# A maximum over partitions moves from two turns on the tensor engine to one instruction on GpSimd

## The chip, the cores and the metric

The kernel runs on one core of one Trainium2 chip. The metric is the time of one execution on the device, in microseconds (us). The kernel before was run three times: 1069.85, 1070.06 and 1070.55 us, median 1070.06. One further execution was taken by the hardware profiler; everything called a row below comes from it.

The engines of a core have short names here: PE is the tensor engine's matrix multiply and PEld its loading of weights, DVE the vector engine, ACT the scalar engine, POOL is GpSimd, SP the engine that issues the transfers. Each works through its own queue in order, and they meet at semaphores.

## What is computed

Two layers over an input of 32 sequences of 256 tokens with 128 channels, all in fp32. Layer 0 is a spin attention gated by a small recurrent feed-forward part. Layer 1 is a retention over 16 heads, gated by a soft mixture of 8 experts with 64 slots each. The change is in the mixture:

```python
logits = jnp.einsum('bnd,esd->bnes', xn, sn)
dispatch = jax.nn.softmax(logits, axis=1)
combine = jax.nn.softmax(logits.reshape(b, n, e * s), axis=-1)
slots = jnp.einsum('bnd,bnes->besd', xn, dispatch)
h = jnp.einsum('besd,edh->besh', slots, w1) + b1[None, :, None, :]
h = jax.nn.gelu(h, approximate=False)
eo = jnp.einsum('besh,ehd->besd', h, w2) + b2[None, :, None, :]
eo = eo.reshape(b, e * s, DIM)
out = jnp.einsum('bmd,bnm->bnd', eo, combine)
```

`combine` is a softmax over the 512 slots of each token, so it needs each token's largest logit.

## The kernel before

**Tiling and stages.** The work is done in 16 pairs of sequences (512 tokens). What a pair needs is cut into named steps, such as `("quad", 3)`, scores of four heads of the retention, or `("h", 5)`, first layer of expert 5. For each of PE, DVE, ACT and POOL the table `ORDER` lists the steps of one turn as (name, index, age). `steps_of` (L226) walks it: in turn t an engine does each listed step for pair t minus age. So one turn holds layer 0 of a new pair (age 0), most of layer 1 of the pair before it (age 1) and the last of layer 1 of the one before that (age 2). There are 18 turns for 16 pairs. The order is fixed when the program is written; at run time an engine only waits on semaphores in that order. The table `BANK` says which of four PSUM banks a step of PE fills.

**The retention's chain.** For each q of 0 to 7: POOL scales the keys (`km`, L320), PE makes the scores (`quad`, L1000 and L1003), DVE applies the causal mask (`ret`, L659), ACT takes the absolute value (`ab`, L479), POOL adds one block onto another (`add`, L326), and PE multiplies with the values (`g`, L1023, done for two q at a time: `g` 4 and `g` 5 stand side by side, 24 matrix instructions each in the trace). `ms` (L1030) follows. There are two buffers of `ret` and `ret_abs`, and four of `km`.

**The mixture.** PE makes the logits with slots on partitions and tokens along the row: four tiles `LT` (L930), which ACT copies to `cT` (`LTc`, L440). The dispatch softmax goes `DTe` (ACT, L455), `drec` (DVE, L723), `dn` (POOL, L333), `DT` (four turns on PE, L952), `Dc` (ACT). Then `slots` (L960), and for each expert `h` (L969), `hb` (DVE), `hg` (ACT, Gelu, L474) and `eo` (L979).

**The token maximum.** In `cT` the slots of a token lie across partitions and over the four tiles. DVE takes the maximum of the four tiles (`mx`, three instructions, L707). To get over the partitions, PE turns the result, four instructions (`mxT`, L938), DVE reduces each row and negates it (`rmax`, L712), PE turns it back spread over all partitions, four instructions (`rB`, L945), and ACT copies it out of PSUM (`rBc`, L445). DVE adds it to each tile (`cs`, L719), ACT takes the exponential (`ce`, L449), and `out` (L989) uses it. `out` waits for `ce` 3.

**Layer 0.** Between these stand `s` (L845), `k` (L890), `global` (L840), `score` (L856, two), `r` (L884), `PT` (L866, two), `srow` (L825), `v` (L896), `local` (L876). POOL makes the reciprocal roots of the layer norms (`rstd`, `rstd2`, `rnorm`), with a power instruction each; `xn2T` on PE waits for `rstd2` over DVE's `xn2`.

## Time and profile before

| | |
|---|---|
| median of three runs | 1070.06 us |
| the profiled execution's own time | 1069.8 us |
| its span, first to last instruction | 1068.0 us |
| busy PE / PEld | 1040.6 / 822.9 us |
| busy DVE / ACT / POOL | 918.3 / 810.7 / 414.8 us |
| mean granted clock of the tensor engine | 0.996 of full |

The span is what the rows are measured in; 1.8 us of the execution lie outside it. Busy time counts the instructions that compute. Matrix instructions overlap on PE, and the profile models their ends, so their durations add up to more than they take: the spacing of their starts, or the pieces of the chain of waits, tell what one step costs. The steady part of the execution repeats itself to within some hundredths of a microsecond from pair to pair.

### The profile page before, as it was taken

The numbers are of one execution on the slowest core, as the hardware profiler recorded it, in microseconds if no ns is written. First come the engines' busy times: TensorE is split into PE (matmuls) and PEld (weight loads), VectorE is DVE, ScalarE is ACT, GpSimd is POOL, SyncE is SP. The second block draws the span as 40 slices with busy tenths as digits, with TensorE's granted clock in tenths as the row PEclk, the third lists the DMA queues.
The fourth block names the chain that finished last, engine by engine and source line by source line (L and its number), as shares of the span: only waits on it lengthen the run. The fifth ranks groups of instructions, "written<-read, shape, count | busy, mean of one in ns | idle before, by whom it ended". The sixth has DMA issues, their size and how long they took to land.

```text
span 1068.0 us, 27273 instructions
## 1 busy us (share of the span) xinstructions
PE 1040.6 (97%) x10244; PEld 822.9 (77%) x10244; DVE 918.3 (86%) x1818; ACT 810.7 (76%) x1434; POOL 414.8 (39%) x555
## 2 busy tenths in 40 slices
...
DMA packets 18463, 16.85 MB, mean 16 GB/s; under 512 B 800, under 2 KB 17440, under 8 KB 18080
## 3 DMA queue, kind: packets, MB, share of 16 engines
...
## 4 chain that ended last, share of the span: by engine, by line
PE 94%; DVE 2%; issue 1%; ACT 1%; POOL 0%; DVEq 0%; ACTq 0%; POOLq 0%
PE bank L1023 13%; PE bank L979 11%; PE bank L969 11%; PE bank_s L1000 7%; PE bank L989 6%; PE bank L960 5%; PE bank L930 5%; PE bank L825 3%; PE bank L856 3%; PE bank L923 3%; PE bank L910 3%; PE bank L952 3%; PE bank_s L1003 3%; PE bank L876 3%; PE bank L1030 3%; PE bank L1038 2%
## 5 line engine op out<-in xcount | busy, mean ns | idle before, releaser
L326 POOL TENSOR_TENSOR ret_abs<-ret_abs 128x512 f32<-128x512 f32 x128 | 181.4, 1421 | 250.5 <-ACT ret_abs L479 250.3
L659 DVE TENSOR_TENSOR ret<-bank_s,k_sb 128x1536 f32<-128x1536 f32 x128 | 223.7, 1748 | 29.5 <-PE bank_s L1003 19.9
L479 ACT ACTIVATE ret_abs<-ret 128x1536 f32<-128x1536 f32 x128 | 189.7, 1482 | 26.8 <-DVE ret L659 26.8
L979 PEld LDWEIGHTS bank<-w_sb,hact 128*128 128x128 f32 x1024 | 127.9, 191 | 18.0 <-issue 7.8
L979 PE MATMUL bank<-w_sb,hact 128*128 128x128 f32 x1024 | 138.6, 278 | 0.0
L333 POOL TENSOR_SCALAR dT<-dT,drec 128x256 f32<-128x256 f32 x128 | 67.2, 542 | 170.2 <-DVE drec L723 170.2
L969 PE MATMUL bank<-slotsT,w_sb 128*128 128x128 f32 x1024 | 130.1, 275 | 0.4 <-ACT slotsT L469 0.4
L969 PEld LDWEIGHTS bank<-slotsT,w_sb 128*128 128x128 f32 x1024 | 123.2, 192 | 1.7 <-ACT slotsT L469 0.8
L474 ACT ACTIVATE hact<-hact 128x512 f32<-128x512 f32 x128 | 80.1, 627 | 52.1 <-DVE hact L728 51.8
L1023 PE MATMUL bank<-ret,vrow 128*32 128x256 f32 (+1 forms) x2048 | 108.2, 329 | 0.3 <-POOL ret_abs L326 0.3
L1000 PE MATMUL bank_s<-qT,km 32*128 32x256 f32 x1024 | 91.4, 426 | 0.9 <-POOL km L320 0.6
L1023 PEld LDWEIGHTS bank<-ret,vrow 128*32 128x32 f32 x2048 | 59.9, 109 | 42.0 <-issue 2.5
L728 DVE TENSOR_TENSOR hact<-bank,v_sb 128x512 f32<-128x512 f32 x128 | 87.4, 683 | 4.5 <-PE bank L969 2.4
L320 POOL TENSOR_SCALAR km<-kT,k_sb 128x256 f32<-128x256 f32 x128 | 76.1, 606 | 37.5 <-DVE kT L645 37.5
L1023 PE MATMUL bank<-ret_abs,k_sb 128*32 128x256 f32 x1024 | 78.7, 379 | 0.0
L455 ACT ACTIVATE dT<-cT,ltmax 128x256 f32<-128x256 f32 x128 | 63.8, 505 | 7.1 <-PE bank L952 5.9
L1000 PEld LDWEIGHTS bank_s<-qT,km 32*128 32x128 f32 x1024 | 40.0, 182 | 37.5 <-issue 32.6
L440 ACT ACTIVATE cT<-bank 128x512 f32<-128x512 f32 x64 | 38.4, 600 | 35.7 <-PE bank L989 27.5
L989 PE MATMUL bank<-eorow,cT 128*128 128x129 f32 x512 | 61.4, 278 | 1.0 <-issue 1.0
L989 PEld LDWEIGHTS bank<-eorow,cT 128*128 128x128 f32 x512 | 58.4, 191 | 3.0 <-issue 1.2
L739 DVE TENSOR_TENSOR eorow<-bank,v_sb 64x256 f32<-64x256 f32 x128 | 53.6, 419 | 5.5 <-PE bank L979 4.5
L960 PE MATMUL bank<-d,xn 128*128 128x512 f32 x128 | 57.7, 593 | 0.0
...
## 6 DMA issues: line engine op xcount, KB each, us to landing
...
w_sb<-w SPq DMA_DIRECT2D x2, 2048.0 KB, 13.8
...
k_sb<-consts SPq DMA_DIRECT2D x1, 538.0 KB, 5.9
...
```

The source lines that it names most:

```text
L320: pool.tensor_scalar(km[:, q % KM], kT[par][:, b], K["head"][:, i:i + 1], 1.0, ALU.mult, ALU.mult)\
L326: pool.tensor_tensor(both[:, :, P:SEQ], both[:, :, P:SEQ], both[:, :, SEQ:3 * P], ALU.add)\
L474: act.activation(hact[:, e % 2], hact[:, e % 2], ACT.Gelu).then_inc(ready["hg"].sem, 1)
L479: act.activation(ret_abs[:, q % MR], ret[:, q % MR], ACT.Abs).then_inc(ready["ab"].sem, 1)
L659: dve.tensor_tensor(ret[:, q % MR], bank_s[:, :, 0:3 * P], causal.unsqueeze(1).broadcast_to([P, Q, 3 * P]), ALU.mult)\
L728: dve.tensor_tensor(hact[:, e % 2], bank[:].rearrange("p (c n) -> p c n", c=HC), V["b1"][:, e * HC:(e + 1) * HC].unsqueeze(2).broadcast_to ...
L960: ins = pe.matmul(bank[:], xn3[:, j], d[:, j], start=(i == 0), stop=(i == 1))
L969: ins = pe.matmul(bank[:, c * P:(c + 1) * P], w1_sb[:, e, c * P:(c + 1) * P], slotsT[:, e // 2, 2 * (e % 2):2 * (e % 2) + 2].rearrange("p ...
L979: ins = pe.matmul(bank[:, i * C:(i + 1) * C], hact[:, i, c], w2_sb[:, e, c], start=(c == 0), stop=(c == HC - 1))
L989: ins = pe.matmul(bank[:, i * (C + 1):(i + 1) * (C + 1)], cT[:, m, j * P:(j + 1) * P], eorow[:, m, b], start=(m == 0), stop=(m == E // 2 - 1))
L1000: pe.matmul(bank_s[:, n, 0:SEQ], km[rows, q % KM, 0:P], qT[par][rows, b], start=True, stop=True)
L1023: ins = pe.matmul(bank[n * HT:(n + 1) * HT, into[0]:into[1]], left, src[:, q % MR, n, cols[0]:cols[1]], start=(i == 0 and phase == 0), sto ...
```

## The change

GpSimd takes the maximum over partitions itself. In the function `rBc`, now on POOL, `partition_all_reduce` writes to every partition of `rB` the maximum over the 128 partitions of `mx`.
```diff
--- before.py
+++ after.py
 ORDER = {
...
-    "POOL": [("rnorm", 0, 1), ("add", 6, 2), ("add", 7, 2), ("rstd", 0, 0), ("km", 0, 1), ("km", 1, 1),
...
+             ("km", 5, 1), ("add", 2, 1), ("km", 6, 1), ("km", 7, 1), ("add", 3, 1), ("rBc", 0, 1), ("add", 4, 1),
+             ("add", 5, 1), ("rstd2", 0, 0), ("rnorm", 0, 0), ("add", 6, 1)],
...
@@ -139,7 +139,7 @@
         snT_turned = slot_sb[:].rearrange("p j c -> p (j c)")
         slot_n = sb("slot_n", 3, 4)
         mu1, gamma2, warm = sb("mu1", 2), sb("gamma2", 1), sb("warm", 1)
-        mhalf, ln_eps = sb("mhalf", HEADS), sb("ln_eps", TILES)
+        mhalf, ln_eps, spare = sb("mhalf", HEADS), sb("ln_eps", TILES), sb("spare", 2)
         W = {n: w_sb[:, a:b] for n, (a, b) in W_COLS.items()}
         V = {n: v_sb[:, a:b] for n, (a, b) in V_COLS.items()}
         K = {n: k_sb[:, a:b] for n, (a, b) in K_COLS.items()}
@@ -180,7 +180,7 @@
 
         cT = sb("cT", 4, TOK)
 
-        mx, rmax, rB = sb("mx", TOK), sb("rmax", TILES), sb("rB", TOK)
+        mx, rB = sb("mx", TOK), sb("rB", TOK)
         crec = sb("crec", TILES)
         ltmax, dsum, drec = sb("ltmax", 4, 2), sb("dsum", 4, 2), sb("drec", 4, 2)
         dT, d = sb("dT", 2, 2, SEQ), sb("d", TILES, ES)
@@ -326,6 +326,15 @@
                 pool.tensor_tensor(both[:, :, P:SEQ], both[:, :, P:SEQ], both[:, :, SEQ:3 * P], ALU.add)\
                     .then_inc(ready["add"].sem, 1)
 
+            def rBc(p, par, k):
+
+
+                pool.partition_all_reduce(spare[:, 0:1], mhalf[:, 0:1], P, bass.bass_isa.ReduceOp.max)
+                pool.wait_ge(*ready["mx"](p, 2))
+                since(pool, ready["cs"], p - 1, 3)
+                pool.partition_all_reduce(rB[:], mx[:], P, bass.bass_isa.ReduceOp.max).then_inc(ready["rBc"].sem, 1)
+                pool.tensor_tensor(spare[:, 1:2], mhalf[:, 0:1], mhalf[:, 0:1], ALU.add)
+
             def dn(p, par, m):
                 pool.wait_ge(*ready["drec"](p, m))
                 pool.sem_inc(passed["gpsimd"].sem, 1)
@@ -344,7 +353,7 @@
                 pool.tensor_tensor(slot_n[:, 2], slot_n[:, 1], mhalf[:, 0:4], ALU.pow).then_inc(ready["slot_rn"].sem, 1)
 
             steps_of({"rstd": rstd_, "mixa": mixa, "rstd2": rstd2_, "rnorm": rnorm_, "km": km_,
-                            "add": add, "dn": dn}, ORDER["POOL"],
+                            "add": add, "rBc": rBc, "dn": dn}, ORDER["POOL"],
                      between={("rstd", 0): derived, ("mixa", 0): slot_norms})
 
         @block.scalar
@@ -439,11 +448,6 @@
                 since(act, filled["out"], p - 1, 1)
                 act.activation(cT[:, m], bank[:], ACT.Copy).then_inc(ready["LTc"].sem, 1)
 
-            def rBc(p, par, k):
-                bank = bank_of("rB", p)
-                since(act, ready["cs"], p - 1, 3)
-                act.activation(rB[:], bank[:], ACT.Copy).then_inc(ready["rBc"].sem, 1)
-
             def ce(p, par, m):
                 act.wait_ge(*ready["cs"](p, m))
                 act.activation(cT[:, m], cT[:, m], ACT.Exp).then_inc(ready["ce"].sem, 1)
@@ -514,7 +518,7 @@
                         .then_inc(ready["slot_ready" if j < 3 else "slot_sqs"].sem, 1)
 
             steps_of({"xnTc": xnTc, "sT": sT_, "sgT": sgT_, "eTc": eTc, "P": P_, "PTc": PTc, "sp": sp_, "tr": tr, "kr": kr, "tv": tv,
-                           "xn2Tc": xn2Tc, "xn3Tc": xn3Tc, "LTc": LTc, "rBc": rBc, "ce": ce, "DTe": DTe, "Dc": Dc, "slc": slc,
+                           "xn2Tc": xn2Tc, "xn3Tc": xn3Tc, "LTc": LTc, "ce": ce, "DTe": DTe, "Dc": Dc, "slc": slc,
                            "hg": hg, "ab": ab, "gTb": gTb, "usq": usq_, "dsq": dsq, "ln": ln, "rs": rs, "zt": zt_}, ORDER["ACT"],
                      between={("eTc", 0): slot_squares})
 
@@ -701,22 +705,16 @@
             def mx_(p, par, i):
                 dve.wait_ge(*ready["LTc"](p, i + 1))
                 if i == 0:
-                    since(dve, filled["mxT"], p - 1)
+                    since(dve, ready["rBc"], p - 1)
                 else:
                     dve.wait_ge(*ready["mx"](p, i - 1))
                 dve.tensor_tensor(mx[:], mx[:] if i else cT[:, 0], cT[:, i + 1], ALU.max).then_inc(ready["mx"].sem, 1)
-
-            def rmax_(p, par, k):
-                bank = bank_of("mxT", p)
-                since(dve, filled["rB"], p - 1)
-                dve.tensor_reduce(rmax[:], bank[:].rearrange("p (j s) -> p j s", j=TILES), X, ALU.max, negate=True)\
-                   .then_inc(ready["rmax"].sem, 1)
 
             def cs(p, par, m):
                 dve.wait_ge(*ready["rBc"](p))
                 dve.wait_ge(*ready["DTe"](p, m))
                 dve.wait_ge(*ready["mx"](p, 2))
-                dve.tensor_tensor(cT[:, m], cT[:, m], rB[:], ALU.add).then_inc(ready["cs"].sem, 1)
+                dve.tensor_tensor(cT[:, m], cT[:, m], rB[:], ALU.subtract).then_inc(ready["cs"].sem, 1)
 
             def drec_(p, par, m):
                 dve.wait_ge(*ready["DTe"](p, m))
@@ -791,7 +789,7 @@
             steps_of({"stat": stat_, "xn": xn_, "mix": mix_, "gbias": gbias_, "srowc": srowc, "smax": smax_,
                            "srec": srec_, "field": field, "ka": ka_, "rv": rv_, "rvg": rvg, "prod": prod, "x1": x1_,
                            "stat2": stat2_, "xn2": xn2_, "xn3": xn3_, "qkc": qkc, "vgc": vgc, "ret": ret_, "den": den_, "ug": ug_,
-                           "rx": rx_, "gated": gated_, "attn": attn_, "LTm": LTm, "mx": mx_, "rmax": rmax_, "cs": cs, "drec": drec_, "hb": hb, "eoc": eoc,
+                           "rx": rx_, "gated": gated_, "attn": attn_, "LTm": LTm, "mx": mx_, "cs": cs, "drec": drec_, "hb": hb, "eoc": eoc,
                            "z": z_, "zg": zg, "sg": sg, "x2": x2_}, ORDER["DVE"],
                      between={("stat", 0): derived, ("smax", 1): slots_scaled, ("stat2", 0): slots_turned})
 
@@ -930,20 +928,6 @@
                     ins = pe.matmul(bank[:, b * SEQ:(b + 1) * SEQ], (snT[:], snT_turned)[b][:, m * P:(m + 1) * P],
                                     xn3T[:, b * SEQ:(b + 1) * SEQ], start=True, stop=True)
                 ins.then_inc(filled["LT"].sem, 1)
-
-            def mxT(p, par, k):
-                pe.wait_ge(*ready["mx"](p, 2))
-                bank = claim("mxT", p)
-                for j in range(TILES):
-                    ins = pe.transpose(bank[:, j * P:(j + 1) * P], mx[:, j * P:(j + 1) * P], ident)
-                ins.then_inc(filled["mxT"].sem, 1)
-
-            def rB_(p, par, k):
-                pe.wait_ge(*ready["rmax"](p))
-                bank = claim("rB", p)
-                for j in range(TILES):
-                    ins = pe.transpose(bank[:, j * P:(j + 1) * P], rmax[:, j:j + 1].broadcast_to([P, P]), ident)
-                ins.then_inc(filled["rB"].sem, 1)
 
             def DT(p, par, m):
                 pe.wait_ge(*ready["dn"](p, m))
@@ -1054,7 +1038,7 @@
 
             steps_of({"xnT": xnT_, "s": s, "global": global_, "e": e, "srow": srow_, "score": score, "PT": PT,
                           "local": local, "r": r, "k": k_, "v": v, "xn2T": xn2T_, "xn3T": xn3T_, "qk": qk, "vg": vg, "LT": LT,
-                          "mxT": mxT, "rB": rB_, "DT": DT, "slots": slots, "h": h, "eo": eo, "out": out_, "quad": quad, "g": g,
+                          "DT": DT, "slots": slots, "h": h, "eo": eo, "out": out_, "quad": quad, "g": g,
                           "gT": gT, "ms": ms, "o": o}, ORDER["PE"],
                      between={("s", 0): weights_in, ("local", 0): slots_across, ("xn2T", 0): slots_in})
 
```

What moved, in the order of instructions. POOL, middle of a steady turn: `km`, `add` and `dn` of one pair before the change.

```order
L320 TENSOR_SCALAR km<-kT,k_sb 128x256 x2
L326 TENSOR_TENSOR ret_abs<-ret_abs 128x4x128 x2
L333 TENSOR_SCALAR dT<-dT,drec 128x256 x2
L326 TENSOR_TENSOR ret_abs<-ret_abs 128x4x128 x2
L320 TENSOR_SCALAR km<-kT,k_sb 128x256
L299 TENSOR_TENSOR var_eps<-mv,ln_eps 128x4
L301 TENSOR_TENSOR rstd<-var_eps,mhalf 128x4
```

The same place after the change. The two ISA rows without operands load a library; the one with `spare` is the one-column reduction.

```order
L320 TENSOR_SCALAR km<-kT,k_sb 128x256 x2
L326 TENSOR_TENSOR ret_abs<-ret_abs 128x4x128
L332 ISA
L332 ISA spare<-mhalf 128x1
L335 ISA rB<-mx 128x512
L336 ISA
L336 TENSOR_TENSOR spare<-mhalf 128x1
L326 TENSOR_TENSOR ret_abs<-ret_abs 128x4x128 x2
L299 TENSOR_TENSOR var_eps<-mv,ln_eps 128x4
L301 TENSOR_TENSOR rstd<-var_eps,mhalf 128x4
L306 TENSOR_TENSOR rn<-rstd 128x4
```

The reduction and its two library loads now stand between `add` 3 and `add` 4 of a pair, once for each pair; all `km` and `dn` of the pair stand ahead of them, and `add` 4, `add` 5, `rstd2` and `rnorm` behind.

PE before the change, from `g` 0 and `g` 1 over `quad` 3 to `ms` 0.

```order
L1023 MATMUL bank<-ret_abs,k_sb 32x256 x4
L938 MATMUL bank<-k_sb,mx 128x128 x4
L845 MATMUL bank<-sT,w_sb 128x512
L890 MATMUL bank<-mix,w_sb 128x512
L1000 MATMUL bank_s<-qT,km 128x256 x4
L1003 MATMUL bank_s<-qT,km 128x128 x4
L952 MATMUL bank<-k_sb,dT 128x128 x4
L945 MATMUL bank<-k_sb,rmax 128x128 x4
L1030 MATMUL bank<-usq,k_sb 128x256
```

PE after the change, from `local` (L874 now) over `quad` 5 (L984, L987), `ms` 1 (L1014), four steps each of `h` (L953) and `eo` (L963), `quad` 6, to `g` 4 (L1007).

```order
L874 MATMUL bank<-srow,probT 128x128 x8
L984 MATMUL bank_s<-qT,km 128x256 x4
L987 MATMUL bank_s<-qT,km 128x128 x4
L1014 MATMUL bank<-usq,k_sb 128x256
L953 MATMUL bank<-slotsT,w_sb 128x128 x4
L963 MATMUL bank<-w_sb,hact 128x128 x8
L953 MATMUL bank<-slotsT,w_sb 128x128 x8
L963 MATMUL bank<-w_sb,hact 128x128 x8
L984 MATMUL bank_s<-qT,km 128x256 x4
L987 MATMUL bank_s<-qT,km 128x128 x4
L1007 MATMUL bank<-ret,vrow 32x256 x4
```

The turns by L938 and L945 are gone. Between `quad` 3 and `g` 4 of a pair PE now has `vg` 1, `h` 2 to 4 and `eo` 0 to 3 more than before, and `DT` 1, `rB`, `o` 1 and `global` less.

On DVE and ACT, `cs` and `ce` 1 to 3 have moved from the end of a pair's age-1 turn into its next turn. There PE's order up to `out` is `eo` 5, `h` 7, `ms` 2, `g` 6, `g` 7, `eo` 6, `eo` 7, `ms` 3, `qk` 0, `xn3T`, `qk` 1, and ACT's ends with `hg` 7, `usq` 3, `ce` 1, `dsq` 3, `ce` 2, `ce` 3.

## Rows read from the trace of the kernel before

**Rows 1.** The page: busy time of PE; engines' shares of the chain.

```profile
PE 1040.6 (97%) x10244; PEld 822.9 (77%) x10244; DVE 918.3 (86%) x1818; ACT 810.7 (76%) x1434; POOL 414.8 (39%) x555
...
PE 94%; DVE 2%; issue 1%; ACT 1%; POOL 0%; DVEq 0%; ACTq 0%; POOLq 0%
```

**Rows 2.** Windows, 64 us: busy PE, PEld, DVE, ACT, POOL; clock, DMA.

```profile
454.00:518.00 64.00, 64.00 (x640) 50.80 (x636) 56.85 (x113) 50.00 (x90) 25.85 (x34) 1.00 0.04 10
```

**Rows 3.** Groups of PE: busy us, mean ns of one, idle before.

```profile
L938 PE MATMUL bank<-k_sb,mx 128*128 128x128 f32 x64 | 10.5, 286 | 0.0
```

**Rows 4.** Chain of waits, 504 to 569 us: start, length, step.

```profile
504.83 0.58 PE bank L938 x4
...
507.13 0.65 PE bank_s L1000 x8
...
508.00 0.59 PE bank L952 x4
508.58 0.44 PE bank L945 x4
...
509.89 0.89 PE bank L1038 x8
510.79 0.87 PE bank L856 x4
511.65 0.12 PE bank L840 x2
...
515.90 0.59 PE bank L866 x4
516.49 0.89 PE bank L884 x8
...
524.04 1.78 PE bank L876 x16
...
528.90 2.30 PE bank L1023 x48
531.21 1.09 PE bank L979 x8
532.29 0.89 PE bank L969 x8
...
558.53 0.86 PE bank L916 x4
```

**Rows 5.** Groups of POOL: busy us, mean ns of one, idle before.

```profile
L326 POOL TENSOR_TENSOR ret_abs<-ret_abs 128x512 f32<-128x512 f32 x128 | 181.4, 1421 | 250.5 <-ACT ret_abs L479 250.3
...
L313 POOL TENSOR_TENSOR rnorm<-rn,mhalf 128x4 f32<-128x4 f32 x16 | 16.5, 1031 | 1.3
...
L308 POOL TENSOR_TENSOR rn<-rn,mv 128x4 f32<-128x4 f32 x16 | 3.2, 202 | 1.3
```

**Rows 6.** Timeline of POOL, first turn and a steady one: start, length.

```profile
2.58 0.10 POOL L278 MEMSET xnT<- 128x2 f32 x1
5.31 0.20 POOL L284 TENSOR_TENSOR var_eps<-mv,ln_eps 128x4 f32<-128x4 f32 x1 [2.63 <-DVE mv L539]
...
511.42 1.68 POOL L326 TENSOR_TENSOR ret_abs<-ret_abs 128x512 f32<-128x512 f32 x1 [2.33 <-ACT ret_abs L479]
```

**Rows 7.** Transfers: KB of one, us from issue to landing.

```profile
w_sb<-w SPq DMA_DIRECT2D x2, 2048.0 KB, 13.8
...
k_sb<-consts SPq DMA_DIRECT2D x1, 538.0 KB, 5.9
```

**Rows 8.** Groups of ACT: busy us, mean ns of one, idle before.

```profile
L479 ACT ACTIVATE ret_abs<-ret 128x1536 f32<-128x1536 f32 x128 | 189.7, 1482 | 26.8 <-DVE ret L659 26.8
L474 ACT ACTIVATE hact<-hact 128x512 f32<-128x512 f32 x128 | 80.1, 627 | 52.1 <-DVE hact L728 51.8
...
L474 ACT ACT_TABLE_LOAD x32 | 41.1, 1283 | 0.6
L449 ACT ACTIVATE cT<-cT 128x512 f32<-128x512 f32 x64 | 39.6, 620 | 0.2
...
L493 ACT ACTIVATE den<-den 128x256 f32<-128x256 f32 x64 | 26.3, 410 | 13.2 <-DVE den L666 13.2
```

More of the change, by code:

```diff
@@ L53 @@
 ORDER = {
-    "PE": [("h", 6, 2), ("ms", 2, 2), ("eo", 4, 2), ("h", 7, 2), ("eo", 5, 2), ("xn2T", 0, 1), ("g", 6, 2),
-           ("g", 7, 2), ("xn3T", 0, 1), ("qk", 0, 1), ("qk", 1, 1), ("eo", 6, 2), ("ms", 3, 2), ("eo", 7, 2),
-           ("LT", 0, 1), ("quad", 0, 1), ("out", 0, 2), ("out", 1, 2), ("LT", 1, 1), ("gT", 0, 1), ("xnT", 0, 0),
[3 rows of a table removed]
-           ("score", 0, 0), ("global", 0, 0), ("score", 1, 0), ("quad", 4, 1), ("g", 2, 1), ("g", 3, 1),
[5 rows of a table removed]
-            ("stat", 0, 0), ("ug", 3, 2), ("qkc", 0, 1), ("den", 3, 2), ("qkc", 1, 1), ("xn", 0, 0), ("rx", 3, 2),
-            ("eoc", 3, 2), ("ret", 0, 1), ("z", 0, 2), ("gated", 0, 2), ("z", 1, 2), ("LTm", 0, 1), ("LTm", 1, 1),
-            ("mx", 0, 1), ("vgc", 0, 1), ("drec", 0, 1), ("ret", 1, 1), ("gated", 1, 2), ("attn", 0, 2),
-            ("zg", 0, 2), ("vgc", 1, 1), ("LTm", 2, 1), ("mx", 1, 1), ("mix", 0, 0), ("mx", 2, 1), ("drec", 1, 1),
-            ("drec", 2, 1), ("ret", 2, 1), ("rmax", 0, 1), ("den", 0, 1), ("ug", 0, 1), ("ret", 3, 1),
-            ("rx", 0, 1), ("LTm", 3, 1), ("attn", 1, 2), ("sg", 0, 2), ("gbias", 0, 0), ("smax", 0, 0),
-            ("drec", 3, 1), ("smax", 1, 0), ("ka", 0, 0), ("ret", 4, 1), ("ug", 1, 1), ("srec", 0, 0),
[6 rows of a table removed]
-            ("zt", 0, 2), ("gTb", 0, 1), ("DTe", 0, 1), ("xnTc", 0, 0), ("ab", 0, 1), ("gTb", 1, 1), ("LTc", 2, 1),
-            ("ab", 1, 1), ("DTe", 1, 1), ("LTc", 3, 1), ("DTe", 2, 1), ("sT", 0, 0), ("Dc", 0, 1), ("usq", 0, 1),
-            ("ab", 2, 1), ("eTc", 0, 0), ("kr", 0, 0), ("dsq", 0, 1), ("Dc", 1, 1), ("rBc", 0, 1), ("ab", 3, 1),
-            ("DTe", 3, 1), ("sgT", 0, 0), ("P", 0, 0), ("Dc", 2, 1), ("P", 1, 0), ("usq", 1, 1), ("PTc", 0, 0),
[3 rows of a table removed]
@@ L101 @@
+BANK = {("DT", 0): 0, ("DT", 1): 2, ("DT", 2): 2, ("DT", 3): 0, ("LT", 0): 1, ("LT", 1): 3, ("LT", 2): 2,
[7 rows of a table added]
 READ_BY = {"xnT": ("xnTc", 0), "s": ("sT", 0), "global": ("gbias", 0), "e": ("eTc", 0), "srow": ("srowc", 0),
            "score": "P", "PT": "PTc", "local": ("field", 0), "r": ("tr", 0), "k": ("kr", 0), "v": ("rv", 0),
-           "xn2T": ("xn2Tc", 0), "xn3T": ("xn3Tc", 0), "qk": "qkc", "vg": "vgc", "LT": "LTc", "mxT": ("rmax", 0), "rB": ("rBc", 0), "DT": "Dc", "slots": "slc", "h": "hb", "eo": "eoc", "g": "rx", "gT": "gTb", "o": "attn",
+           "xn2T": ("xn2Tc", 0), "xn3T": ("xn3Tc", 0), "qk": "qkc", "vg": "vgc", "LT": "LTc", "DT": "Dc", "slots": "slc", "h": "hb", "eo": "eoc", "g": "rx", "gT": "gTb", "o": "attn",
```

20 lines of the change are left out of this document (15 added, 5 removed), and 53 rows, old and new, of tables (BANK, ORDER).

## The prediction

> **What bounds the kernel now.** I read the page first. PE is busy 1040.6 of 1068.0 us, and the chain of waits, followed back from the end, lies on PE for 94% [rows 1]. The next question is whether PE's busy time hides waiting. The windows say no: in 64 us of the steady part PE is busy all 64.00, at the full granted clock (1.00), while DVE is busy 56.85, ACT 50.00 and POOL 25.85 [rows 2]. The chain cut into pieces shows one PE step begin as the last ends [rows 4]. So a microsecond taken from PE's steps in every pair comes off 16 times, as long as no other engine becomes late; and POOL has some 38 us free in each pair's 64. The change trades one for the other. The sum is therefore two questions: what PE gets back, and whether POOL's new work fits where it was put.
>
> **What PE gets back.** The group of `mxT` says 286 ns each, four to a pair and 64 in all, 10.5 us [rows 3]. That is not what it costs, since matrix instructions overlap. The chain's pieces are 0.58 us for `mxT` and 0.44 for `rB` [rows 4]. Of the 0.58, some 0.14 is what whatever stands behind a `g` pays: the first `PT` there shows 0.59 as well [rows 4], for four turns like the 0.44 of `rB`. That stays, with another step. So 0.44 + 0.44, and at most 0.58 + 0.44: I take 0.9 us a pair, 16 x 0.9 = **14.4 us** (16.3 at most).
>
> **What else goes.** `rmax` on DVE and the copy on ACT cost nothing now and give nothing: their cover is PE's full turn, and DVE has 7 us and ACT 14 us of every 64 free [rows 2]. `cs` keeps its length, subtract for add. The two bank claims that go, and the new `BANK`, I price at zero.
>
> **What POOL gets.** For each pair: a library load, a reduction of one column, the reduction of 512 columns, a load back, an addition of one column. The small ones are fixed cost, as the 202 ns of an operation on four columns [rows 5]: 0.2 us each, 0.4 together.
>
> The load. The program of before has one, and it must lie between the last memset, which starts at 2.58, and the addition at 5.31, which waited for DVE for its 2.63 us of idle time [rows 6]. 
>
> The reduction. From below it is one pass of 512 columns, 1.42 us for the addition [rows 5]. From above I take the slowest rate of this engine in the trace: the power instruction needs 1031 - 202 = 829 ns more than an addition for the same four columns [rows 5], 207 ns a column, or 106 us for 512. A maximum is as simple as an addition, and nearer to the first. It must be done inside each processor, across the processors, and back: three passes, 3 x 1.42 = **4.3 us**. With a pass for each halving of 128 partitions it would be seven, 9.9 us.
>
> W = two loads and the reduction = 2 x 5.9 + 4.3 = **16.1 us**. POOL's 25.85 a pair becomes 42.4 of 64: it fits by amount. What counts is the place.
>
> **Where it lies on the path.** Queued behind the reduction are `add` 4 and `add` 5; `g` 4 and `g` 5 on PE wait for these. Time 0 is the start of `quad` 3. Before, it starts at 507.13 and `g` 4 at 528.90, 21.8 us later [rows 4]. The new order takes out of that stretch `DT` 1 (0.59), `rB` (0.44), `o` 1 (0.89) and `global` (0.12), and puts in `vg` 1 (0.86, as `gT` and `vg` by L916), three `h` (0.89 each) and four `eo` (1.09 for the first, 0.89 for others, as `h`) [rows 4]: 21.8 - 2.0 + 0.9 + 2.7 + 3.8 = **27.1**. `g` 5 starts half of 2.30 later, at 28.2.
>
> POOL's side: `add` 3 starts at 511.42 and takes 1.68 [rows 6], so it ends 6.0 after `quad` 3. Then 6.0 + 0.4 + 16.1 = 22.5 for the end of the new block, `add` 4 (1.42 [rows 5]) done at 23.9, `add` 5 at 25.3. PE wants them at 27.1 and 28.2: **spare 2.9 us**. So W may be 19.0 before PE waits, and each microsecond over costs 16 us; the gain of 0.9 is used up at W = 19.9. The wait for `mx` inside the block is covered: the last `mx` follows `srow` on PE, about 11 us after `quad` 3, and the first load lasts until 11.9. `cs` 0 alone is needed in that turn, and `rstd2` behind `add` 5 has until `xn2T`, 5 us after `g` 4.
>
> **The last pair.** In turn 17 of 18 no new pair enters, and PE's stretch lacks its layer 0: two `score` (0.87 each), `r` (0.89), two `PT` (0.59 and 0.44), `srow` and `v` (some 0.5 and 0.89), `local` (1.78) [rows 4], 6.8 us. PE is at `g` 4 at 20.3, and `add` 4 is done at 23.9: **3.6 us** come back once. In the first turns all engines wait for each other's results anyway; I put that at zero.
>
> **Sum.** 1069.8 (the profiled execution) - 14.4 + 3.6 = **1059.0 us**. The median of the runs is 0.3 above that execution, which I leave out.
>
> **The rivals.**
> *A. A load costs little*, as the one at the start did. W is at most 2 x 2.6 + 4.3 = 9.5, the last pair loses nothing: 1069.8 - 14.4 = 1055.4, and 1053.5 with the larger gain. For it: [rows 6]. Against: that load displaced nothing. Chance 0.12.
> *B. The block is too long for its place.* With seven passes W = 11.8 + 9.9 = 21.7, 2.7 over. Fifteen pairs lose 2.7 - 0.9 = 1.8 each, the last 3.6 + 5.6 - 0.9 = 8.3: 1069.8 + 27 + 8.3 = 1105. At W = 21 it is 1069.8 + 15 x 1.1 + 7.6 = 1094. It decides at W a little under 19.9, or sooner if `add` 3 is later than before, which the new order of ACT (two `Dc` and `sgT` ahead of `ab` 3) could bring. Nothing in the trace speaks against it but my guess at the passes. Chance 0.20, slower.
> *C. The gain goes into a wait for `ce` 3.* `cs` and `ce` 1 to 3 now stand in the turn in which `out` needs them. From the turn's start PE reaches the end of `g` 7 after two steps of 0.89, `ms` 0.4 and 2.30, 4.5 us; then ACT has `usq` and `dsq` (0.41 each), a table load (1.283) and three exponentials (0.620) [rows 8], 4.0 us, until 8.5. PE is at `out` at about 8.9, with seven short steps. 0.4 us of spare is nothing; one more table load, or `ab` 7 (1.482) coming late, eats the 0.9: about 1070, and with the last pair's 3.6 up to 1073. Chance 0.10, half of it within 0.2%.
> *D. The reduction is slow as such.* The rate would have to be near the power instruction's. At its 106 us W is 117.8, 98.8 over, and the time 1069.8 + 16 x 97.9 = 2636 us: POOL, not PE, sets the pace. [...] Chance 0.03, slower. The Trainium skill (GPSIMD Engine Reference, section 3.2, Cross-partition) speaks against the change here: it gives 247,699 ns for a reduction along the partitions at 128 x 2048, an estimate of 61.9 us for a quarter of the columns, and by it the time would be some 1930 us.
>
> **How the numbers follow.** Forecast 0.55, A 0.12, B 0.20, C 0.10, D 0.03. This kernel can be told from no change beyond about 0.2%, 2.1 us. Faster: 0.55 + 0.12 = 0.67. Within 0.2%: half of C and the strip of B around W = 20, 0.08. Slower: 0.25. The range reaches from A with the larger gain, 1053, to B with W just over 21, 1096. It leaves out D, the worst of B and a gain larger than PE's own steps, less than 2 in 10. Forecast and A alone would be 1053 to 1063.
>
> **What would show it.** Right: the turns of `mx` and `rmax` gone from PE; in a window of the steady part PE still busy throughout; the distance of one step from itself in the next pair 0.9 us shorter; POOL's gap between the end of `add` 3 and the start of `add` 4 about 16.5 us, with the loads showing as idle time without a releaser or as the reduction's length; `g` 4 never behind `add` 4 but in the last pair. B shows as PE idle before `g` 4 (L1007), released by `ret_abs` of POOL, in every pair. C shows as idle time of PE before `out` (L973), released by ACT's `cT`. A shows as a gap under 10 us. I would be wrong altogether if the slower transfers or DVE's work beside the reduction stretched, which no row of before can tell.

## The result, and the profile after

| | before | after |
|---|---|---|
| median of four runs each, side by side | 1070.16 us (1069.85 to 1070.55) | 1085.18 us (1083.21 to 1086.38) |
| the profiled execution's own time | 1069.8 us | 1084.65 us |
| mean granted clock | 0.996 | 0.994 |

The ratio is 1.0139, with a 95% interval of 1.0124 to 1.0154. The change is slower by 15 us. The time lies inside the forecast range; the forecast itself was a gain of 11 us.

The page after. Its first line answers to the first of [rows 1], its second to the chain there:

```profile
PE 1038.6 (96%) x10116; PEld 815.1 (75%) x10116; DVE 915.9 (85%) x1802; ACT 826.6 (76%) x1434; POOL 431.7 (40%) x603
...
PE 77%; DVE 10%; issue 7%; ACT 4%; POOL 1%; DVEq 0%; ACTq 0%; POOLq 0%
```

PE has 128 instructions less and is busy 2.0 us less, yet the span is 14.9 us longer. The chain, which lay on PE for 94%, now passes through DVE, ACT and "issue" for 21%. A window of one pair's length (start and end; busy PE, PEld, DVE, ACT, POOL; clock, DMA share) no longer shows PE full, as [rows 2] did:

```profile
454.00:519.40 65.40, 64.12 (x633) 50.53 (x632) 57.61 (x112) 51.16 (x89) 26.47 (x37) 1.00 0.03 10
```

The distance of `out` from itself in the next pair was 64.43 to 64.48 us in 13 of the 15 distances; the first was 64.70 and the last 53.5. Now the first 14 lie between 65.2 and 65.8, 65.37 in the mean where it was 64.46, and the last is 56.7. That is 14 x 0.91 + 3.2 = 15.9 us. Of the 3.2, 1.8 are no loss: `LT` 0 and `quad` 0 (0.96 and 0.86 us) now stand behind `out` instead of ahead of it, so they are missing from the last distance before the change and not after it. In return the first `out` starts at 99.3 us instead of 101.1. Behind the last `out` come 0.8 more, and the sum is the span's 14.9.

**POOL's block did what was forecast.** POOL's timeline (start, length, idle before), the pair whose `quad` 3 starts at 512.71:

```profile
518.20 1.26 POOL L326 TENSOR_TENSOR ret_abs<-ret_abs 128x512 f32<-128x512 f32 x1 [1.25 <-ACT ret_abs L483]
525.58 0.38 POOL L332 PARTITION_ALL_REDUCE spare<-mhalf  x1 [6.12 <-issue]
525.88 2.17 POOL L335 PARTITION_ALL_REDUCE rB<-mx  x1
534.92 0.45 POOL L336 TENSOR_TENSOR spare<-mhalf 128x1 f32<-128x1 f32 x1 [6.87 <-issue]
535.34 2.51 POOL L326 TENSOR_TENSOR ret_abs<-ret_abs 128x512 f32<-128x512 f32 x2
```

`add` 3 ends at 519.46, the load shows as 6.12 us of idle time without a releaser, the reduction takes 2.17, the load back 6.87, and `add` 5 is done at 537.85, 25.1 us after `quad` 3 began; 25.3 was forecast. `g` 4 starts at 540.4. POOL's waits and groups give the means (the waits: total, times, longest):

```profile
POOL spare L336 <- issue: 115.4, 16, 7.7
...
POOL spare L332 <- issue: 94.6, 16, 6.2
```

```profile
L335 POOL PARTITION_ALL_REDUCE rB<-mx x16 | 32.5, 2033 | 0.0
```

W is 94.6/16 + 2.03 + 115.4/16 = 5.9 + 2.0 + 7.2 = 15.1 us. PE's waits say the same from the other side. All that PE ever waits for POOL's additions is one wait of 0.4 us, which is the last of these rows:

```profile
PE bank L823 <- DVE xn L554: 8.0, 1, 8.0
PE bank L944 <- ACT rt L421: 7.2, 15, 0.5
...
PE bank_s L984 <- DVE ret L663: 1.3, 2, 0.9
...
PE bank L1007 <- POOL ret_abs L326: 0.4, 1, 0.4
```

The first row is the program's start and was there before (7.9 us). The second is new: `slots` 1 waits in 15 pairs for ACT's copy of `r`. Weight loads (PEld) wait as well, among them for `ce` (L453, before `out`) and `hg` (L478, before `eo` 6; the wait for `hg` was 6.6 us before):

```profile
PEld bank L973 <- ACT cT L453: 9.5, 16, 2.4
PEld bank L963 <- ACT hact L478: 9.5, 16, 0.7
```

Summing the distances from each PE step's start to the next shows where the time is (worked out from PE's starts, us a pair, mean of the first 14 distances of `out`):

| steps of PE | before | after |
|---|---|---|
| turns of `mx` and `rmax` | 0.93 | gone |
| two `PT`, with the wait of `slots` 1 behind one | 0.93 | 1.61 |
| eight `h` | 7.34 | 7.79 |
| two `out` | 3.68 | 3.93 |
| `g` ending in `ret_abs` | 3.91 | 4.11 |
| four `ms` | 1.74 | 1.93 |

So 0.93 goes and 1.77 comes; the other steps, some 0.1 longer and some shorter behind new neighbours, nearly cancel. Of the 0.45 at `h`, 0.38 are at `h` 5: `quad` 7 behind it starts when DVE's `ret` 6 ends. The gain is there, and nearly twice of it is lost in steps that the change did not touch but moved.

### The profile page after: what moved, and what is told of

It is laid out like the page before. It is cut to its first block, busy times and chain, and to the rows that moved or that the text cites. A ratio compares the mean times of both kernels' runs of the same rounds, so it can differ in the third digit from the quotient of the medians.

```text
span 1082.9 us, 27065 instructions
## 1 busy us (share of the span) xinstructions
PE 1038.6 (96%) x10116; PEld 815.1 (75%) x10116; DVE 915.9 (85%) x1802; ACT 826.6 (76%) x1434; POOL 431.7 (40%) x603
## 4 chain that ended last, share of the span: by engine, by line
PE 77%; DVE 10%; issue 7%; ACT 4%; POOL 1%; DVEq 0%; ACTq 0%; POOLq 0%
PE bank L963 9%; PE bank L1007 8%; PE bank L953 8%; PE bank_s L984 7%; PE bank L928 5%; PE bank L973 5%; PE bank L823 3%; PE bank L936 3%; PE bank L944 3%; PE bank L1022 3%; PE bank L874 3%; PE bank L908 3%; PE bank L921 3%; PE bank L914 2%; PE bank_s L987 2%
## 5 line engine op out<-in xcount | busy, mean ns | idle before, releaser
L326 POOL TENSOR_TENSOR ret_abs<-ret_abs 128x512 f32<-128x512 f32 x128 | 171.1, 1340 | 113.7 <-ACT ret_abs L483 113.7
L953 PE MATMUL bank<-slotsT,w_sb 128*128 128x128 f32 x1024 | 134.0, 278 | 1.6 <-DVE hact L726 1.6
L953 PEld LDWEIGHTS bank<-slotsT,w_sb 128*128 128x128 f32 x1024 | 123.3, 192 | 16.1 <-issue 15.2
L963 PE MATMUL bank<-w_sb,hact 128*128 128x128 f32 x1024 | 130.3, 278 | 2.2 <-ACT hact L478 0.7
L963 PEld LDWEIGHTS bank<-w_sb,hact 128*128 128x128 f32 x1024 | 120.6, 192 | 11.5 <-ACT hact L478 9.5
L478 ACT ACTIVATE hact<-hact 128x512 f32<-128x512 f32 x128 | 79.7, 628 | 64.4 <-DVE hact L726 61.5
L1007 PE MATMUL bank<-ret,vrow 128*32 128x256 f32 (+1 forms) x2048 | 108.3, 329 | 0.4 <-POOL ret_abs L326 0.4
L726 DVE TENSOR_TENSOR hact<-bank,v_sb 128x512 f32<-128x512 f32 x128 | 84.4, 680 | 11.8 <-PE bank L953 10.6
L984 PE MATMUL bank_s<-qT,km 32*128 32x256 f32 x1024 | 91.4, 426 | 2.8 <-DVE ret L663 1.3
L1007 PEld LDWEIGHTS bank<-ret,vrow 128*32 128x32 f32 x2048 | 59.8, 109 | 44.9 <-issue 5.3
L1007 PE MATMUL bank<-ret_abs,k_sb 128*32 128x256 f32 x1024 | 78.7, 379 | 0.0
L320 POOL TENSOR_SCALAR km<-kT,k_sb 128x256 f32<-128x256 f32 x128 | 60.8, 483 | 27.2 <-DVE kT L649 27.2
L984 PEld LDWEIGHTS bank_s<-qT,km 32*128 32x128 f32 x1024 | 40.4, 183 | 41.4 <-issue 36.7
L944 PE MATMUL bank<-d,xn 128*128 128x512 f32 x128 | 61.2, 602 | 8.0 <-ACT rt L421 7.2
L823 PEld LDWEIGHTS bank<-k_sb,xn 128*128 128x128 f32 x256 | 31.2, 145 | 34.0 <-issue 24.9
```

The lines of the kernel that those rows point to most:

```text
L326: pool.tensor_tensor(both[:, :, P:SEQ], both[:, :, P:SEQ], both[:, :, SEQ:3 * P], ALU.add)\
L478: act.activation(hact[:, e % 2], hact[:, e % 2], ACT.Gelu).then_inc(ready["hg"].sem, 1)
L726: dve.tensor_tensor(hact[:, e % 2], bank[:].rearrange("p (c n) -> p c n", c=HC), V["b1"][:, e * HC:(e + 1) * HC].unsqueeze(2).broadcast_to ...
L944: ins = pe.matmul(bank[:], xn3[:, j], d[:, j], start=(i == 0), stop=(i == 1))
L953: ins = pe.matmul(bank[:, c * P:(c + 1) * P], w1_sb[:, e, c * P:(c + 1) * P], slotsT[:, e // 2, 2 * (e % 2):2 * (e % 2) + 2].rearrange("p ...
L963: ins = pe.matmul(bank[:, i * C:(i + 1) * C], hact[:, i, c], w2_sb[:, e, c], start=(c == 0), stop=(c == HC - 1))
```

## The experiments

The distances of `out` between pairs serve as a second measure throughout, beside the medians. The kernel before, run beside these kernels, had medians of 1070.41, 1070.01, 1070.23 and 1070.33 us.

**1. Is it POOL's block, or the order?** The block is cut down to one addition; the token maximum over partitions is left out.

```diff
-                pool.partition_all_reduce(spare[:, 0:1], mhalf[:, 0:1], P, bass.bass_isa.ReduceOp.max)
...
-                pool.partition_all_reduce(rB[:], mx[:], P, bass.bass_isa.ReduceOp.max).then_inc(ready["rBc"].sem, 1)
-                pool.tensor_tensor(spare[:, 1:2], mhalf[:, 0:1], mhalf[:, 0:1], ALU.add)
+                pool.tensor_tensor(rB[:], mx[:], mx[:], ALU.add).then_inc(ready["rBc"].sem, 1)
```

> Edit: in the changed kernel the step rBc is one elementwise addition on GpSimd (rB = mx + mx). It leaves out the maximum over the partitions, and with it both library loads; GpSimd's block falls from some 16 us to 1.4. Theory BLOCK (the loads and the reduction are too long for their place): the kernel falls to the forecast of the order without waits, 1053 to 1059 us. Theory ORDER (the new order makes PE wait in places that have nothing to do with GpSimd's block): it stays at 1078 to 1085 us. A mean result, 1065 to 1075, would say that GpSimd's block costs through its neighbours.

Measured: 1084.38 us (1083.76 to 1084.75), ratio 1.013 [1.0114, 1.0145]. Distances 65.23, the last one 56.1. `slots` 1 waits as before:

```profile
PE bank L942 <- ACT rt L419: 7.3, 15, 0.5
```

Taking some 15 us of POOL's time out of every pair gains 0.8 us in all. The loss is the order's. In the last distance the block costs 0.6 us (56.7 with it, 56.1 without).

**2. Does the old way, in the new order, show what the turns cost?** The kernel of before with the new `ORDER` and `BANK`; `mxT` behind `g` 3, `rmax` behind `srec`, `rB` behind `h` 1, the copy behind `dsq` 1. (ACT's and DVE's tables get one row each.)

```diff
+ ... ("g", 3, 1), ("mxT", 0, 1), ("h", 0, 1), ("h", 1, 1), ("rB", 0, 1), ("local", 0, 0) ...
```

> Edit: the kernel before (maximum turned on PE twice, no GpSimd block) with the ORDER and BANK tables of the changed kernel; mxT stands behind g 3, rmax behind srec, rB behind h 1, and its copy behind dsq 1. Theory ORDER: the order itself costs some 0.9 us a pair more than the old one apart from the turns, so 1080 to 1100 us (the changed kernel and the turns' 14 us). Theory BLOCK: the order is as good as the old one, 1070 to 1074 us.

Measured: 1101.26 us (1100.63 to 1103.35), 1.0291 [1.0276, 1.0307]; distances 66.42. Against the changed kernel that is 16.1 us, 1.07 a pair. The reduction on POOL is worth about what the forecast gave it (14.4, at most 16.3). By PE's starts the two turns take 0.95 of the 1.07, and `h` 0 and 1 together are 0.24 longer than in the changed kernel, with a wait that comes from the place I gave the turns; other `h` steps, which vary in the changed kernel, take some back. The order, without the new block, costs 31 us, of which that wait is some 4. `slots` 1 waits here as well, 7.3 us in 15 times.

**3. Which steps of the order?** DVE's timeline after holds an operation twice its usual length. `cs` 1 (L717), beside `add` 7 on POOL:

```profile
549.19 1.38 DVE L717 TENSOR_TENSOR cT<-cT,rB 128x512 f32<-128x512 f32 x1
550.61 1.29 DVE L726 TENSOR_TENSOR hact<-bank,v_sb 128x512 f32<-128x512 f32 x2
```

```profile
548.75 1.28 POOL L326 TENSOR_TENSOR ret_abs<-ret_abs 128x512 f32<-128x512 f32 x1 [2.00 <-ACT ret_abs L483]
```

`cs` 1 stands ahead of `hb` 6 and 7, for which `hg` 6 and `eo` 6 wait. The first kernel moves it behind them. The second also moves ACT's `tr`, the copy of `r`, ahead of the second `P`, so that bank 3 is free sooner for `slots` 1.

```diff
-    "DVE": [("eoc", 2, 2), ("cs", 1, 2), ("hb", 6, 2), ("hb", 7, 2), ("xn3", 0, 1),
+    "DVE": [("eoc", 2, 2), ("hb", 6, 2), ("hb", 7, 2), ("cs", 1, 2), ("xn3", 0, 1),
...
-            ("P", 0, 0), ("P", 1, 0), ("tr", 0, 0), ("PTc", 0, 0),
+            ("P", 0, 0), ("tr", 0, 0), ("P", 1, 0), ("PTc", 0, 0),
```

> Edit: on DVE cs 1 stands behind hb 6 and hb 7 instead of ahead of them. In the changed kernel's trace cs 1 takes 1.38 us instead of 0.68 while GpSimd does add 7, and hb 6, hg 6, then eo 6 on PE wait for it. Theory ORDER: PE's waits at eo 6 (0.2 to 0.3 us a pair) and at out (0.27) go, 4 to 9 us off: 1076 to 1081. Theory BLOCK: no change, 1085.

Measured: 1077.17 us (1076.87 to 1077.44), 1.0062 [1.0045, 1.0079]; most distances 64.75. No `cs` takes more than 0.69 us now, so the move did two things: it took `cs` 1 out of the way of `hb` 6 and away from `add` 7. This run does not tell them apart.

> Edit: cs 1 behind hb 7 on DVE as above, and on ACT tr stands between the two P instead of behind them, so that slots 1, which claims the PSUM bank that tr reads, need not wait for the second P. Theory ORDER: the wait at slots 1 (0.62 us a pair) goes as well, together 14 to 18 us off: 1067 to 1071. Theory BLOCK: no change, 1085.

Measured: 1066.78 us (1066.05 to 1069.12, nine runs), 0.9971 [0.9961, 0.9981]; the shortest distances 64.02. PE's waits have lost the row of `slots` 1. Two moved steps take 18.4 us off the changed kernel and put it ahead of the one before, by 0.3%. The wait of `quad` 7 for `ret` 6 is still there, and larger:

```profile
PE bank_s L986 <- DVE ret L665: 6.0, 11, 0.9
```

**4. And the old order with the new way?** POOL's block in `ORDER` and `BANK` of before, between `dn` 3 and `add` 4.

```diff
-             ... ("add", 3, 1), ("rBc", 0, 1), ("add", 4, 1) ...
+             ... ("dn", 3, 1), ("rBc", 0, 1), ("add", 4, 1) ...
```

> Edit: the new way (maximum over partitions on GpSimd, no turns on PE) with the ORDER and BANK tables of the kernel before; rBc stands between dn 3 and add 4 on GpSimd. By the forecast's rule g 4 starts 20.8 us after quad 3 there, while add 4 is done 7.7 + 0.4 + 15.1 + 1.3 = 24.5 us after it: 3.7 us of waiting less 0.9 gained, times 16 = 45 us more than before, 1110 to 1125 us. If the order had no part in making room, 1057.

Measured: 1188.06 us (1187.0 to 1192.08), 1.1108 [1.1088, 1.1129], clock 0.955. The expectation missed by 63 us or more: it had priced only `add` 4 waiting. There `cs` 0 stands soon behind `mx` on DVE, and DVE waits for POOL, and PE for DVE:

```profile
DVE cT L719 <- POOL rB L337: 102.7, 16, 7.0
...
PE bank L946 <- DVE srow L575: 81.5, 15, 6.0
```

The wait is not the whole of it. `slots` 0, the first step behind it (L946), takes 3.45 us in most pairs for 1.72 before. In a steady pair PE stood for 5.4 us ahead of it, and the windows show a granted clock of 1.00 up to the wait, 0.52 in the 3.5 us behind it (TensorE's lower level, 1.2 of 2.4 GHz) and 1.00 again after that. Of the 7.6 us by which a pair is longer than before, some 5.6 are the wait and 1.7 the clock. So the new order does something for its price: it makes room for the block. The parts of it that cost are others.

**5. `ret` 6 earlier.** From the last good kernel, `hb` 4 goes ahead of `stat2`, and `eoc` 1 behind `ret` 6.

```diff
-            ("x1", 0, 0), ("stat2", 0, 0), ("eoc", 1, 1), ("hb", 4, 1), ("ret", 6, 1), ("xn2", 0, 0),
+            ("x1", 0, 0), ("hb", 4, 1), ("stat2", 0, 0), ("ret", 6, 1), ("eoc", 1, 1), ("xn2", 0, 0),
```

> Edit: the two moves of c1_both, and on DVE ret 6 one step earlier: hb 4 goes ahead of stat2 and eoc 1 behind ret 6. In c1_both's trace quad 7 on PE waits 0.76 us a pair for ret 6, which stands behind x1, stat2, eoc 1 and hb 4 on DVE. Theory ORDER: that wait goes, 0.5 to 0.76 us x 15 = 8 to 11 us off c1_both's 1066.8: 1055 to 1059 us, the forecast's gain at last. Theory BLOCK is out by e1_no_library for the order as it was; if it holds for what is left, this stays at 1066.

Measured: 1082.64 us (1081.52 to 1083.9), 1.0113 [1.0096, 1.013], distances 65.28. A miss: `quad` 7 hardly waits any more, but 16 us are lost against that kernel. `xn2` (L634) takes 2.15 us, and PE waits for it in every pair (7.2 of the 21.7 us are the program's start, as before). Of the timelines of DVE and POOL, and PEld's waits:

```profile
543.76 2.15 DVE L634 TENSOR_SCALAR xn<-x,mv,rstd 128x128 f32<-128x128 f32 x4
```

```profile
543.27 1.13 POOL L315 TENSOR_TENSOR rnorm<-rn,mhalf 128x4 f32<-128x4 f32 x1
544.56 1.26 POOL L328 TENSOR_TENSOR ret_abs<-ret_abs 128x512 f32<-128x512 f32 x1 [0.15 <-ACT ret_abs L485]
```

```profile
PEld bank L825 <- DVE xn L634: 21.7, 16, 7.2
```

Two POOL instructions lie beside it, a power (L315) and `add` 6 (L328). I first took the power for the cause and moved `rnorm` behind `add` 6:

```diff
-             ("rstd2", 0, 0), ("rnorm", 0, 0), ("add", 6, 1)],
+             ("rstd2", 0, 0), ("add", 6, 1), ("rnorm", 0, 0)],
```

> Edit: c2_ret6_early with rnorm behind add 6 on GpSimd (it stood ahead). In c2_ret6_early xn2 on DVE (four operations, SBUF to SBUF) took 2.15 us instead of 1.11, while GpSimd did the power instruction of rnorm (1.13) and then add 6 (1.26); xn2T on PE then waited 0.4 us and eo 4 ended late. Theory PORT (such DVE operations stand still while a GpSimd instruction runs, so the new order's cost is where the two engines' instructions fall on each other): with rnorm out of the way xn2 meets add 6 alone, and 8 to 16 us come off: 1066 to 1074, under 1060 if add 6 misses xn2 as well. Theory ORDER without PORT (ret 6's new place starves xn2 or hb 5 by itself): no change, 1082.

Measured: 1084.27 us (1083.68 to 1084.43), 1.0129 [1.0113, 1.0144]. That reading falls: `xn2` still takes 2.14 us, now with `add` 6 alone beside it, and ends when `add` 6 does:

```profile
543.88 2.14 DVE L634 TENSOR_SCALAR xn<-x,mv,rstd 128x128 f32<-128x128 f32 x4
```

```profile
544.67 1.26 POOL L328 TENSOR_TENSOR ret_abs<-ret_abs 128x512 f32<-128x512 f32 x1 [2.59 <-ACT ret_abs L485]
```

**6. The collision by itself.** In one execution, behind the end of the program, DVE runs eight small operations four times: beside seven additions of 128x512 on POOL, seven powers of four columns, seven one-operand multiplications, and alone. The outputs of the kernel stay; its time of 1109.2 us holds the added part and is not compared.

```diff
+                        ins = pool.tensor_tensor(pr[:, i], mx[:], rB[:], ALU.add)
...
+                        ins = pool.tensor_tensor(pr[:, i, 0:4], ln_eps[:], mhalf[:, 0:4], ALU.pow)
...
+                        ins = pool.tensor_scalar(pr[:, i], mx[:], mhalf[:, 0:1], 1.0, ALU.mult, ALU.mult)
```

> Edit: the changed kernel with a probe behind its end: four times the same seven DVE operations (negation of two columns, addition of two SBUF tiles 128x512, the same with one operand in PSUM, the two-scalar operation 128x128, a maximum along the row from SBUF, and additions again), first while GpSimd does seven additions of 128x512, then seven powers of four columns, then seven one-operand operations of 128x512, then nothing. Theory PORT: the DVE operations that read SBUF alone take up to one GpSimd instruction longer in the first two or three rounds than in the last (0.68 becomes 1.3 to 2.0 us), the one with an operand in PSUM and the row maximum do not. Without PORT all four rounds agree within 0.05 us an operation.

DVE's and POOL's timelines, beside the additions:

```profile
1079.68 9.85 POOL L249 TENSOR_TENSOR w_sb<-mx,rB 128x512 f32<-128x512 f32 x7 [15.80 <-DVE small L259]
1080.04 0.68 DVE L261 TENSOR_TENSOR w_sb<-bank,rB 128x512 f32<-128x512 f32 x1
1080.64 0.69 DVE L262 TENSOR_SCALAR small<-mx,mhalf 128x128 f32<-128x128 f32 x1
1081.25 0.67 DVE L263 TENSOR_REDUCE small<-mx 128x2 f32<-128x512 f32 x1
1081.85 1.17 DVE L264 TENSOR_TENSOR w_sb<-mx,rB 128x512 f32<-128x512 f32 x1
1082.94 1.22 DVE L265 TENSOR_SCALAR small<-mhalf 128x2 f32<-128x2 f32 x1
```

Alone, the last two take 0.68 and 0.17; beside the powers nothing changes (L265 again), and beside one-operand multiplications L265 takes 0.58:

```profile
1092.29 0.18 DVE L265 TENSOR_SCALAR small<-mhalf 128x2 f32<-128x2 f32 x1
...
1099.92 0.58 DVE L265 TENSOR_SCALAR small<-mhalf 128x2 f32<-128x2 f32 x1
...
1104.96 0.34 DVE L262 TENSOR_SCALAR small<-mx,mhalf 128x128 f32<-128x128 f32 x1
...
1105.81 0.68 DVE L264 TENSOR_TENSOR ret_abs<-mx,rB 128x512 f32<-128x512 f32 x1
1106.40 0.17 DVE L265 TENSOR_SCALAR small<-mhalf 128x2 f32<-128x2 f32 x1
```

A DVE operation on SBUF alone was held up here by up to 1.05 us, nearly the length of one two-operand addition of POOL (1.25); the one that reads PSUM (L261), and the row maximum (L263), were not. L262 and L265 end within 0.08 us of the end of one of POOL's additions. L266, an addition of 0.68 us, only seems to have escaped. POOL's records one by one show the hold-up on its side as well: beside L260, L264 and L266 its additions took 1.57, 1.70 and 1.77 us instead of 1.25, and the one of 1.77 began 0.02 us behind L266. Of its one-operand multiplications, 0.69 us each, two took 1.2. Each of these cases was seen once.

**7. `xn2` before the collision.** The same kernel as in 5, with `eoc` 1 behind `xn2`, so that `xn2` is over when `add` 6 starts.

```diff
-            ("ret", 6, 1), ("eoc", 1, 1), ("xn2", 0, 0),
+            ("ret", 6, 1), ("xn2", 0, 0), ("eoc", 1, 1),
```

> Edit: c2_ret6_early with eoc 1 on DVE behind xn2 as well, so that xn2 follows ret 6 at once. In c2_ret6_early and c3_rnorm_late xn2 took 2.15 us instead of 1.11, both times with its last operations ending when add 6 on GpSimd did; the probe says that powers of four columns hold nothing up and additions of 512 columns do. Theory PORT: xn2 now ends some 0.4 us before add 6 starts, takes 1.1 us, xn2T and eo 4 on PE no longer wait, and the time drops by 14 to 20 us against c2_ret6_early's 1082.6, to 1055 to 1066. If it stays at 1078 or more, the collision is not the cause.

Measured: 1067.18 us (1066.5 to 1067.56, six runs), 0.9971 [0.9958, 0.9983]; most distances 64.13. One step moved gives 15.5 us back, as forecast, though the time lies 1 us above the range named, and `xn2` has its length again:

```profile
535.21 1.11 DVE L634 TENSOR_SCALAR xn<-x,mv,rstd 128x128 f32<-128x128 f32 x4
```

The move also starts `xn2` 0.88 us earlier, which by itself would have ended nearly all of the wait. The starts tell which was the cause of the loss. Counted from `quad` 3, `xn2` in experiment 5 runs from 30.97 to 33.12 and `xn2T` starts at 33.17. Here `xn2T` starts at 32.24, straight behind `eo` 4. At its own length of 1.11 `xn2` would have been done at 32.08 there, in time. So the stretch of 1.04 us is the wait of 0.93, some 14 of the 15.5 us.

**8. The block in better orders, and a longer block.** Three kernels with the block cut down as in 1 (the maximum over partitions left out), in the orders of 3 (both moves), 5 and 7; and the kernel of 5 with five powers of four columns added to the block.

```diff
+                for i in range(5):
+                    pool.tensor_tensor(spare[:, 4 + 4 * i:8 + 4 * i], ln_eps[:], mhalf[:, 0:4], ALU.pow)
```

> Edit: c1_both (the good order, 1066.8 us) with rBc as one elementwise addition; leaves out the maximum over the partitions and both library loads. It prices GpSimd's block where the order is good. If the block costs nothing there: 1066. If only the uneven length of the loads costs (periods of 64.3 to 64.8 among ones of 64.02): 1061 to 1064. If PORT holds, the missing block also moves the collisions, and the result can lie some us on either side.

Measured: 1064.79 us (1064.49 to 1064.93), 0.9947 [0.9931, 0.9964]. With the block it was 1066.78: the block costs 2.0 us. Without it all but a few distances are 64.01 or 64.02; with it many are 64.3 to 64.8.

> Edit: c2_ret6_early with rBc as one elementwise addition (leaves out the maximum over the partitions and both library loads). In c1_both some pairs took 0.3 to 0.8 us more than the 64.02 of most, in e1_no_library all took 65.23. If only the varying length of the loads costs something once the order is good, this is 2 to 5 us under c2_ret6_early; if GpSimd's block costs nothing, the same.

Measured: 1084.09 us (1083.97 to 1084.69), 1.0131 [1.0116, 1.0146], against 1082.64 with the block: nothing gained.

> Edit: c4_xn2_first with rBc as one elementwise addition (leaves out the maximum over the partitions and both library loads). c1_no_library was 2.0 us under c1_both, and all its periods alike; the same 2 to 4 us are expected here, and up to 6 if the tighter order has less room for long loads.

Measured: 1066.72 us (1066.43 to 1067.3), 0.9967 [0.9954, 0.998], against 1067.18: no difference that can be told, where 2 to 4 us were expected.

> Edit: c2_ret6_early with five power instructions of four columns (1.03 us each, 5.15 us) added to the end of GpSimd's block, ahead of add 4. The forecast's rule says that add 4 and add 5 have some 2.6 us to spare (c1_both: add 4 done at 528.7, g 4 at 531.45) and each microsecond over costs 16 us: (5.15 - 2.6) x 16 = 41 us more than c2_ret6_early. If other steps behind the block (rstd2, rnorm, add 6) bind sooner it is up to 80; under 10 if the block has more room than thought.

Measured: 1121.83 us (1120.55 to 1126.56), 1.049 [1.0467, 1.0514], 39.2 over the kernel of 5. With 5.15 us more and 2.6 of spare, the rule of the forecast gives (5.15 - 2.6) x 16 = 41. The sum agrees partly by luck: the distances are 2.0 us longer than in 5 in the steady pairs and 7.1 in the last, where the rule has the same for all. At 2.0 a pair, with 4.97 us for the five powers in the trace, the spare was 3.0. The wait that the forecast named for a block too long is there: PE stood ahead of `g` (L1011) for POOL's additions 16 times, 33.9 us in all, and the weight loads wait too:

```profile
PEld bank L1011 <- POOL ret_abs L328: 46.6, 41, 5.4
```

## Why the forecast missed

- **What PE gets back: right.** 0.93 us a pair by PE's starts, 1.07 between the two ways in the same order (with a wait in it, see 2), for 0.9 taken.
- **W: right in sum, by errors that cancel.** The first load is 5.9 as taken, the load back 7.2 instead of 5.9, the reduction 2.0 instead of 4.3: 15.1 for 16.1. The Trainium skill (GPSIMD Engine Reference, section 2.1, Instruction dispatch) puts the first call after a load at about 6 us; these rows agree for one library, and show 7.2 for the other. The Trainium skill's figure for a reduction along the partitions (GPSIMD Engine Reference, section 3.2, Cross-partition), from which I had the estimate of 61.9 us, is not borne out for this instruction: 2.03 us in the row of L335.
- **The place and the spare: right, with small errors that cancel.** `add` 5 was done 25.1 us after `quad` 3, for 25.3: `add` 3 ended at 6.75 instead of 6.0, and the block and the two additions were shorter. `g` 4 started at 27.7, for 27.1. The longer block put the spare at 3.0, for 2.9. With this, B (too long) and D (slow) are out as causes, and A (cheap loads) too, since both loads cost 6 and 7 us.
- **C, a wait for `ce` 3: half true.** PEld waits for it, and the two `out` are 0.25 us a pair longer. It is one of five places, and alone would have left a gain.
- **The last pair: wrong.** 3.6 us of waiting for `add` 4 were forecast, and PE waited 0.4. Without the block it came to `g` 4 21.9 us after `quad` 3, not 20.3. With it `add` 4 was done at 22.3, not 23.9, and `g` 4 started at 22.4. Between kernels with and without the block the last distance differs by 0.2 to 0.8 us. That it grew by 3.2 is near the forecast by accident: 1.8 of them are the new place of `out`.
- **The step that failed** is the condition under the first sum, "as long as no other engine becomes late", with the sentence "The two bank claims that go, and the new `BANK`, I price at zero". I put the time of moved steps into the spare for POOL, and, but for C and the steps behind POOL's block, never asked of a moved step who waits for it. Four had no room. `slots` 1 takes the bank of `r` in both kernels, but six steps of PE stood between them and now two, while ACT's `tr` stands behind both `P`: 0.59 us at `PT` 0. `cs` 1 stands ahead of `hb` 6: 0.20 at `g` 7. `ce` 1 to 3 stand ahead of `out`: 0.25. `ret` 6 stands behind `eoc` 1 and `hb` 4: 0.38 at `h` 5. That is 1.4 of the 1.77 us a pair, against the 0.93 gained; the rest is in pieces of 0.1 and less, for which no row shows a wait. Moving two steps again brought 18.4 us.
- **The second fault is under it.** I took DVE's durations from the trace of before as fixed, and thought of a stretch only beside the reduction, as something "which no row of before can tell". The collision is with additions that POOL had all along, and the trace of before shows it: in each of 15 pairs one `cs` (L719) took 1.13 us, the others 0.68, and after the change one in each of 16 pairs took 1.32 to 1.44. Among DVE's groups `snmax`, two columns, took 304 ns in the mean before and 572 after. What mattered was whether the stretched operation was one that PE waits for. Of the timeline of before:

```profile
526.90 1.13 DVE L719 TENSOR_TENSOR cT<-cT,rB 128x512 f32<-128x512 f32 x1
```

```profile
526.21 1.27 POOL L326 TENSOR_TENSOR ret_abs<-ret_abs 128x512 f32<-128x512 f32 x1 [3.13 <-ACT ret_abs L479]
```

Open: the good orders run at 64.02 and 64.13 us a pair at best, 64.31 and 64.18 in the mean of the first 14 distances, where before less PE's gain would be 63.5. That is why the best kernel, 1066.78, is not 1059. The difference is spread over `h`, `out` and `ms`; I did not take it apart, nor test what the reduction itself does to DVE.
